# A gated delta rule kernel: its 64 recurrence turns written out in place of a hardware loop, and the output norm's sums of squares kept in PSUM

## The reference, cut to what matters

```python
def step(state, inp):
    q_t, k_t, v_t, b_t, g_t = inp
    state = state * jnp.exp(g_t)[..., None, None]
    for j in range(nh):
        kj = k_t[:, j]
        corr = jnp.einsum('bhk,bhkv->bhv', kj, state)
        u = (v_t[:, j] - corr) * b_t[:, j][..., None]
        state = state + jnp.einsum('bhk,bhv->bhkv', kj, u)
    o_t = jnp.einsum('bhk,bhkv->bhv', q_t, state)
    return (state, o_t)
...
o = o * jax.lax.rsqrt(jnp.mean(o * o, axis=-1, keepdims=True) + EPS)
o = o * norm_w * jax.nn.silu(gate)
```

## Time and profile before

| | |
|---|---|
| median of 3 runs | 4071.66 us |
| the profiled execution's own time | 4081.52 us |
| its span | 4079.2 us |
| granted TensorE clock, mean | 0.969 |
| instructions | 108406 |

### The profile page before, as it was taken

How to read it: one execution, slowest core, us unless ns; L and a number is a source line. 1 busy time by engine, 2 the same in 40 slices (tenths; PEclk the granted TensorE clock), 3 DMA queues, 4 the chain that set the end, 5 groups by cost and what they waited for, 6 DMA issues and landing times. The chain is left out here.

```text
span 4079.2 us, 108406 instructions
## 1 busy us (share of the span) xinstructions
PE 3818.6 (94%) x38395; PEld 3178.8 (78%) x38395; DVE 2784.4 (68%) x7247; ACT 2235.5 (55%) x6182; POOL 1585.1 (39%) x2837
## 2 busy tenths in 40 slices
PE   6699999999999999999996899799999999999899
PEld 5588887888878888788885898678887877877678
DVE  5577777777777777777773553577767676676564
ACT  2466666666667666666662443444444444444354
POOL 0567777777777777677761000000000000000010
PEclk9999999999999999999996999899999999999999
DMA  4333333333333333333332320211111111110110
GB/s 172 117 88 87 104 98 106 86 92 111 95 98 94 98 105 88 105 96 104 88 94 83 123 86 33 82 51 34 56 40 52 40 56 48 44 57 29 37 54 31
DMA packets 543243, 322.34 MB, mean 79 GB/s; under 512 B 251744, under 2 KB 501088, under 8 KB 541024
## 3 DMA queue, kind: packets, MB, share of 16 engines
q1 hardware_dynamic: 542688, 315.21, 26.6%
HBM read 231.00 MB, written 84.01 MB: 77 GB/s over the span
## 5 line engine op out<-in xcount | busy, mean ns | idle before, releaser
L1038 DVE SCALAR_TENSOR_TENSOR g_conv<-g_r,g_taps,g_conv 128x511 f32<-128x511 f32 (+2 forms) x961 | 713.8, 743 | 27.2 <-issue 8.0
L2075 ACT ACTIVATE a_pr<-a_pr,a_low 128x128 f32<-128x128 f32 (+3 forms) x512 | 287.0, 561 | 470.8 <-DVE a_low L2221 455.6
L2376 POOL TENSOR_TENSOR a_dg<-a_const,a_fl 128x384 fp32r<-128x384 f32 x32 | 26.5, 828 | 1151.0 <-DVE a_fl L2228 1151.0
L2221 DVE CUSTOM_DVE_ANT_0 a_pr<-a_sc,a_bias 128x128 f32<-128x128 f32 (+3 forms) x512 | 241.5, 486 | 186.7 <-issue 168.8
L604 PE MATMUL g_r<-g_x_hi,g_w_hi 128*128 128x512 f32 x646 | 316.1, 489 | 11.6 <-issue 10.9
L901 ACT ACTIVATE g_us<-g_chn 128x128 f32<-128x128 f32 x528 | 146.8, 278 | 286.0 <-PE g_chn L710 282.5
L1902 PE MATMUL a_out<-a_pt,a_v 128*128 128x512 f32 (+3 forms) x1024 | 297.9, 434 | 0.9 <-DVE a_oT L2241 0.9
L1224 POOL TENSOR_TENSOR g_prod<-g_small 64x14 f32<-64x14 f32 (+6 forms) x896 | 228.8, 255 | 140.6 <-DMA g_small<-lower_d 75.1
L1226 POOL TENSOR_TENSOR g_small<-g_small,g_prod 64x14 f32<-64x14 f32 (+6 forms) x896 | 242.9, 271 | 70.6 <-POOL g_prod L1224 0.7
L1902 PEld LDWEIGHTS a_out<-a_pt,a_v 128*128 128x128 f32 x1024 | 185.0, 191 | 103.1 <-issue 62.5
L1066 DVE SCALAR_TENSOR_TENSOR g_R<-g_chn,g_ctab,g_bv 128x128 f32<-128x128 f32 x462 | 161.1, 349 | 147.6 <-PE g_chn L703 135.1
(11 more groups left out here) (378 smaller groups left out, 11516.3 us busy)
## 6 DMA issues: line engine op xcount, KB each, us to landing
g_w_raw<-w_heads SPq DMA_DIRECT2D x66, 768.0 KB, 4.4
lower_d<-g_L SPq DMA_DIRECT2D x64, 512.0 KB, 3.2
g_U<-upp_d SPq DMA_DIRECT2D x64, 512.0 KB, 5.1
a_w<-w_groups SPq DMA_DIRECT2D x32, 640.0 KB, 4.4
oT_d<-g_oT SPq DMA_DIRECT2D x67, 256.0 KB, 4.9
g_T<-low_d SPq DMA_DIRECT2D x64, 256.0 KB, 3.0
g_T<-low_d SPq DMA_DIRECT2D x128, 128.0 KB, 3.3
f_oT<-oT_d SPq DMA_DIRECT2D x8, 2048.0 KB, 8.3
```

The lines of the kernel that those rows point to most:

```text
L1038: ins = V.scalar_tensor_tensor(out=y[:, k:L], in0=x[:, 0:L - k], scalar=tap, in1=y[:, k:L], op0=ALU.mult, op1=ALU.add)
L2075: A(pr[g % 2][:, i, 0:width(i)], pr[g % 2][:, i, 0:width(i)], ACT.Exp, scale=-1.0, bias=low[g % 2][:, i:i + 1], accum_out=tot[g % 2][:, i: ...
L2221: V.tensor_tensor_reduce(pr[g % 2][:, i, 0:width(i)], sc[i % 2][:, 0:width(i)], bias[tp_][:, i, 0:width(i)], -SCALE, 3.0e38, ALU.add, ALU. ...
```

## The change

`units` loses its hardware loop: all 64 turns are written out for all five engines, with numbers in place of registers. `j` becomes `b % 2`, which is the same value. No turn gains, loses or moves an engine operation. The tile `oss` is no more a tile of its own in SBUF: it is now the first four columns of the unused fourth tile of the PSUM bank `chn`. ACT's read of the accumulator writes there, and DVE's `oden` reads from there. The change takes one line out, so lines behind it are one lower in the changed kernel (L603 is L604 of before).

```diff
-        oss, oden, osd, orec = (sb(f"g_{n}", [P, TT]) for n in ("oss", "oden", "osd", "orec"))
+        oden, osd, orec = (sb(f"g_{n}", [P, TT]) for n in ("oden", "osd", "orec"))
...
         chn = ps("g_chn", [P, TT, P])
         ob = ps("g_ob", [P, TT, P])
+        oss = chn[:, TT - 1, 0:TT]
...
         def units(eng, turn):
 
-            with eng.Fori(0, B // 2) as i:
-                for j in (0, 1):
-                    b = i * 2 + j
-                    for hp in range(H // QN):
-                        for q in range(QN):
-                            turn(b * H + hp * QN + q, q, b * (H // 2) + hp * (QN // 2) + q // 2, b, hp, j)
+            for b in range(B):
+                for hp in range(H // QN):
+                    for q in range(QN):
+                        turn(b * H + hp * QN + q, q, b * (H // 2) + hp * (QN // 2) + q // 2, b, hp, b % 2)
...
-                V.scalar_tensor_tensor(out=oden[:], in0=oss[:], scalar=1.0 / P, in1=qden[(q + 2) % QN][:], op0=ALU.mult, op1=ALU.add).then_inc(s["d_oden"], 1)
+                V.scalar_tensor_tensor(out=oden[:], in0=oss, scalar=1.0 / P, in1=qden[(q + 2) % QN][:], op0=ALU.mult, op1=ALU.add).then_inc(s["d_oden"], 1)
```

## The result

Twenty runs of the changed kernel have a median of 4066.57 us (4056.99 to 4080.61). The kernel before has a median of 4091.9 us in twenty runs, the three shown at first among them: 20 us over their median. The ratio is 0.9941, with a 95% interval of 0.9925 to 0.9958: 0.59% faster. The ratio goes by fast runs, and one run of before, of 4251.43 us, was a slow one. The profiled execution took 4065.73 us, its span is 4063.9 us, and 100531 instructions are left of 108406.

The account below looks back on a forecast made before the run. PE, busy 94% of the span, was taken as the bound. Terms -16.3 - 3 - 4 + 1 = -22.3 us gave 4049.4 from the 4071.7 median, said as 4050 us, 0.53% less; range 4032 to 4067.

Parts of the forecast that it names:

- The three taken branches: PE's three loop ends, some 3.8 us standing each plus lower clock, become quiet turns: -16.3 us.
- The cover that I named for the other engines: At the loop ends other engines branch too, but PE's gap covers them; no size of its own.
- The gaps in the dense piece: PE's stalls at fetch packet ends among the small matmuls (L635, L644, L650) stay but move: -3 us, ends -10 and +12.
- 57.0 / 24 = 2.4 us a gap: Price per gap in PE's dense piece: the 57.0 us over quiet turns and loop ends, shared among 24 gaps.
- The register instructions: On every engine they go; most cost nothing, 0.01 us at each of 14 steps a turn at most: -4 us.
- The sums of squares in PSUM: DVE's `oden` reading PSUM takes 217 ns of fixed cost against 160; +1 us taken, ends -2 and +3.8.
- Behind the stage: Behind the delta rule no instruction changes, but packet ends shift: 0 with 6 us either way.
- the shorter turn: Rival: register instructions hold up dispatch at many more places, the stage loses a further 15 us: 4035; chance 0.12.
- the gaps are the loop's own: Rival: stalls in the dense piece come from the loop's passes and all go: about 4000; chance 0.04.
- The dearer norm: Rival: ACT's four reads each cost as much more as DVE's one, 17 us or so beyond +1: 4067; chance 0.08.
- The moved gap: Rival: at the loop's end a late fetch remains, 3.8 us become 1, some -10: 4062; chance 0.09.
- The packets that lock on the dense piece: Rival: packet ends match every second turn, 32 turns stall where 20 did: +39, or 4111 us; chance 0.07.

Follow-up runs that it names:

- psum_only: The kernel before, its loop kept, with only the sums of squares moved to PSUM: 4073.49 us, ratio 0.9953 to the kernel before.
- unroll_only: The changed kernel with the sums of squares back in SBUF, all turns written out: 4122.99 us, ratio 1.0065 to the kernel before.
- packets_in: The changed kernel with 39 tiny PE matmuls ahead of the stage and three more PE waits a turn: 4134.75 us, ratio 1.0099 to the kernel before.
- the two packet kernels: The changed kernel with three more PE waits a turn and 39 or 55 tiny matmuls ahead of the stage: 4134.75 us and 4048.82 us.

## Where the prediction failed, and where it held

The forecast was 0.53% less, by -22.3 us, and the measurement is 0.59% less, some 24 us. As a time it was 4050, and 4066.57 came, 0.4 us inside the upper end of 4032 to 4067: the median of before, 4071.7 in three runs, is 4091.9 in twenty. That the difference came out is luck. Two mechanisms were missing from the sum, the wait that moves onto a table load and the hold by POOL. In the profiled executions the register instructions, forecast at -4, measured +19, and the gaps, forecast at -3, measured -22; these two misses cancel.

**The three taken branches, -16.3.** This held. No gap stands at the projection any more. The cover that I named for the other engines holds as long as PE branches too, and costs 9 us without it.

**The gaps in the dense piece, -3.** The mechanism was right, in more detail than hoped: 893 a turn, a stall where a packet lies inside (or nearly), 22 gaps where 20 to 28 were said, in every second turn over most of the stage, and two kernels that turn them off and on. What failed was "at 57.0 / 24 = 2.4 us a gap". It put all 57 us down to packets, at one price. A part, some 10 us of DVE's time, was `oden`, held by POOL, and the late `on` behind it. And the price is not one: a gap is 0.3 to 1.2 us long and costs 0.5 to 1.4 us at full clock, and up to 3.8 where the clock falls. The earlier trace rows had it in plain sight: 1493 ns as the longest of 66 whose median is 164, and the earlier trace rows has `on` late by up to 2.3 us. I read the median and left the maximum. The item measured -22: the first two turns are 5 us shorter, the gaps are 4.7 us shorter in sum, and of turns with a gap eight in place of ten came at the lower clock. How much of it is the missing hold stays open, as psum_only, without the hold, still has 56.0 us in this item.

**The register instructions, -4.** This step failed by its sign: +19, and +21 by unroll_only alone (30.62 us for 30.30). I priced what register instructions cost, and said of waits only that one "moved to an instruction of its own" stands where the register instruction stood. The case that came is the other one: the wait moved on to a neighbour, a table load that used to run early. The upper bound of this step was 0; a loss had been left out with no reason given.

**The sums of squares in PSUM, +1.** This step failed too, by its price and by what it left out. `oden` takes 162 ns from PSUM, not 217. The nearest rows misled, since they were of 128 and 511 columns, and a line through two sizes says little about four columns. The Trainium skill's 65 ns for VectorE on PSUM (Perfetto Trace Analysis, Optimizing Scalar/DVE Operations) is not seen here either. ACT's accumulator reads became shorter, 186 ns in the median for 216, and the squares beside them longer, 322 for 283. In the quiet turn it comes to 0.05 us less (30.25 in psum_only). And the main effect, the hold by POOL, was not among the terms: up to some 19 us by psum_only's median, and some 50 in the straight kernel.

**Behind the stage, 0 with 6 either way.** 6 more in the profiled execution, at the edge, and 4 less in the second one.

Of the rivals, the shorter turn fell, as the quiet turn grew. That the gaps are the loop's own fell with the 22 gaps; that they fell at the same turns in each pass is what packets counted from the branch give as well. The dearer norm fell with 162 ns. The moved gap fell with PE's waits: none stands at the projection. The packets that lock on the dense piece did not happen, but packets_in shows that the rival was a real one, with its place and nearly its price: 31 gaps in every second turn, and slower than before by 1% (it had said 32 and 4111; the run gave 4134.75 beside 4088.76).

## What to carry to other kernels

Look at the maximum of a short instruction beside its median: a four-column DVE operation that once takes nine times its usual time is being held, and two SBUF operands beside a busy POOL are the first suspect; with one of them in PSUM this instruction was never held again, though `bk`, with two in SBUF, still was. When register instructions or other fillers go, list which waits they carried and what now carries them, above all where a table load stands ahead of an activation. And where a piece of code is dense enough to outrun its fetch, count its place in the packets: here 16 tiny matmuls ahead of a stage were worth 2%.

## What the runs showed of the hardware that was not expected

A DVE instruction with two operands in SBUF was held for up to 4.83 us, over four POOL instructions that each took about 1 us, and not only over the one that was running when it came. With POOL's list straight it was held longer (mean 702 ns) than with POOL in the loop (437, and 315 in the kernel before); why, the traces don't show.

A table load of 1283 ns carries a wait of the activation that it serves, and then starts late with it.

PE's fetch could not always follow 338 instructions in 3.3 us: a gap of 0.3 to 1.2 us where a packet of 256 has 239 or more of its instructions in them, and none of 0.3 us in this piece otherwise. Every such gap stands at the same place of 256 in PE's list, 1.2 to 1.7 us behind the landing of a 16.4 KB transfer. That straight code without a branch stalls is what the kernel before showed and the two packet kernels prove.
